# Inverse roots of the keys' norms from GpSimd to ScalarE, context rows all normalised on GpSimd, with a new order table for every engine, in a two-block attention network

## The chip, the cores and the metric

The kernel runs on one core of a Trainium2 chip. The metric is the device time of one execution in microseconds (us). Four compute engines run side by side, each through its own queue in order: TensorE (PE), VectorE (DVE), ScalarE (ACT) and GpSimd (POOL). SyncE (SP) issues the DMAs. Engines wait for one another on semaphores.

## The reference

The input `x` is 512 tokens (8 batches of 64) of width 128, with a context of 8 x 1601 rows of width 128. Six blocks follow one another, each added to `x` after a layer norm:

1. `_L0_xattn_ref`: four layers of self-attention, cross-attention to the first context rows, and a gated feed-forward part.
2. `_L0_attn_ref`: messages, with a sigmoid of pairwise products.
3. `_L0_ffn_ref`: one small product.
4. `_L1_xattn_ref`: the tokens attend to the 1601 context rows of their batch and to themselves.
5. `_L1_attn_ref`: causal attention with rotary positions.
6. `_L1_ffn_ref`: eight experts, all computed, two kept per token.

The change is in `_L1_xattn_ref`. What it needs of the context rows:

```python
xn = layernorm(x, ln_x_g, ln_x_b)          # x is the context here: (row - mean) * rsqrt(var + eps)
kv = jnp.concatenate([xn @ W_kv, ln @ W_kv], axis=1)
kn = rmsnorm(k, k_gamma)                   # k / max(norm(k) / 8, 1e-8) for each of 2 heads of 64
sim = einsum(qn, kn); masked; attn = softmax(sim); out = attn @ v
```

## The kernel before, in words

All work is cut into named pieces. Token tiles are t = 0..3 (128 tokens each). A context batch i = 0..7 has thirteen tiles of 128 rows, in groups g = 0..3 of 4, 4, 4 and 1 tiles (`CG`). In a piece's name the first number is the layer, batch or expert and the second the tile or group. The table `PIECES` says which engine runs a piece, and the table `PLACES` gives each piece its place in that engine's queue: `Order` sorts by it, and the engine runs the pieces one after another. `PLACED` gives the PSUM bank of each PE piece, and `WARM` the number of matmuls on a zero tile (L727) that PE runs ahead of a piece. A piece waits for others by `after(engine, od, piece, i, g)`, and `step` makes an engine wait for its own last instruction. Layer 4 of `turn1`, `project`, `scores` and so on is the attention of `_L1_attn_ref`.

For one context batch the chain of pieces is:

- DVE `c_moments` (mean and variance of each row, done during the layers, L1507 and L1510), then POOL `c_power` (L1719 to L1722: 1/sqrt(var + eps) and minus mean times that).
- POOL `c_normed` (groups 0 and 1, L1733 and L1735) and ACT `c_spread` (groups 2 and 3, one ACTIVATE for each of five tiles, L1291) write the normalised rows to `xh[i % 3]`. Both wait until `sum_ctx` of batch i-3 has read that buffer.
- PE `c_turn` (transposes, L1061), ACT `c_turned` (L1301), PE `c_keys` (L1067), ACT `c_squares` (L1307), DVE `c_sums` (L1514), POOL `c_rnorm` (L1738 and L1739): the inverse norm of every key in `rk`. Beside it PE `c_scores` (L1077 and L1079), which needs `c_turned` only.
- DVE `c_scaled` multiplies scores by `rk` (L1518), DVE `c_top` and `top` take the maximum over the batch (L1525 to L1538), PE `top_turn` (L1085), DVE `top_row` and `top_diag` (L1541, L1545), PE `top_spread` (L1089), DVE `shifted` (L1550), ACT `weights` (exponential, L1311), PE `sum_ctx` (weighted sum of `xh`, L1094), then `u_turn` and `heads`.

`load_context` loads batch b (SP) when `c_normed` and `c_spread` of batch b-2 are through. The rule that decides whether a piece is the first of its kind:

```python
def leads(od, p, i, g):
    if SHAPE[p][1] == T:
        return (p, i, g) in od.first
```

`od.first` holds the earliest group of each piece and batch, and T is 4.

## Time and profile before

| | us |
|---|---|
| median of 3 runs | 488.76 (488.09 to 489.97) |
| the profiled execution, its own time | 495.46 |
| its span from first to last instruction | 493.5 |
| PE busy | 455.0 (92%) |
| DVE busy | 366.1 (74%) |
| ACT busy | 280.3 (57%) |
| POOL busy | 217.8 (44%) |

The busy time of an engine is the sum of its instructions' durations. The span is cut three ways below: layers and most of the messages up to 280 us, context and the causal attention up to 430 us, the experts after that. A clock of 1.00 is TensorE at its higher level, 2.4 GHz, and 0.50 is 1.2 GHz. "POOL rk L1739" is the pow instruction that writes tile `rk`.

### The profile page before, as it was taken

To read this page: it belongs to the slowest core of one execution; us is meant where nothing else is said; L and a number is where in the kernel's file an instruction comes from. 1 tells how busy PE (TensorE), PEld (TensorE's weight loads), DVE (VectorE), ACT (ScalarE), POOL (GpSimd) and SP (SyncE) were. 2 spreads that over 40 slices of the span, in tenths; PEclk is the share of its full clock that TensorE was granted. 3 is DMA by queue.
4 is the path that set the end of the run, shared out by engine and by line. 5 is a ranking of instruction groups with operands and counts; after the bars stand their busy time and mean duration, and the time that the engine had idled before them with its cause. 6 is when DMAs were issued, how large, how long until landed. Compare 5 with 4: busy or idle time off the path is not lost.

```text
span 493.5 us, 14858 instructions
## 1 busy us (share of the span) xinstructions
PE 455.0 (92%) x5683; PEld 392.6 (80%) x5705; DVE 366.1 (74%) x1053; ACT 280.3 (57%) x752; POOL 217.8 (44%) x350
## 2 busy tenths in 40 slices
PE   8998998999879989999789999978999899999997
PEld 3666876777769767889779899867889798789996
DVE  5888899669874897565752669978788996865553
ACT  3688487767766787662562544836657644443131
POOL 4703474534452475211652449966667751110000
PEclk9999799999988998999989999979999999999999
DMA  7921222030201400000420037030100000000000
GB/s 206 386 83 41 68 79 66 3 107 20 98 30 35 139 3 2 2 3 3 149 70 1 4 114 298 17 117 2 68 2 2 0 1 1 3 1 4 0 2 26
DMA packets 10321, 27.84 MB, mean 56 GB/s; under 512 B 1391, under 2 KB 5381, under 8 KB 9990
## 3 DMA queue, kind: packets, MB, share of 16 engines
q1 hardware_dynamic: 10246, 26.82, 16.1%
q8 instruction: 49, 0.80, 0.7%
q14 instruction: 26, 0.21, 0.1%
HBM read 26.55 MB, written 0.26 MB: 54 GB/s over the span
## 4 chain that ended last, share of the span: by engine, by line
PE 58%; DVE 20%; POOL 8%; ACT 6%; issue 6%; DMA 1%; SPq 0%; DVEq 0%; POOLq 0%; ACTq 0%
PE ps L1164 6%; PE ps L1155 6%; PE ps L1008 3%; PE ps L1094 3%; PE ps L939 3%; PE ps L879 3%; PE ps L1079 3%; PE ps L972 2%; POOL rk L1739 2%; PE ps L869 2%; PE ps L1067 2%; DVE mx L1381 2%; POOL rsx L1720 2%; PE ps L999 2%; DVE own L1386 2%
## 5 line engine op out<-in xcount | busy, mean ns | idle before, releaser
L1682 POOL TENSOR_TENSOR rstd<-ss,par 128x1 f32<-128x1 f32 x52 | 28.7, 557 | 60.0 <-ACT sq L1184 59.9
L1739 POOL TENSOR_TENSOR rk<-rk,par 128x8 f32<-128x8 f32 (+1 forms) x32 | 46.0, 1438 | 2.7
L1212 ACT ACTIVATE own<-own 128x512 f32<-128x512 f32 x56 | 35.2, 628 | 17.4 <-DVE own L1412 8.7
L1381 DVE TENSOR_REDUCE mx<-ps 128x8 f32<-128x512 f32 x40 | 27.3, 682 | 5.0 <-PE ps L861 4.7
L1079 PE MATMUL ps<-own,xnT 128*128 128x128 f32 x208 | 29.6, 282 | 0.9 <-DVE ssq L1486 0.3
L1164 PE MATMUL ps<-we,own 128*128 128x128 f32 x256 | 30.3, 276 | 0.0
L1672 POOL TENSOR_TENSOR qk<-own 128x128 f32<-128x128 f32 x40 | 18.6, 470 | 25.9 <-DVE own L1374 25.4
L1164 PEld LDWEIGHTS ps<-we,own 128*128 128x128 f32 x256 | 29.7, 192 | 0.4
L1155 PE MATMUL ps<-hT,we 128*128 128x256 f32 x128 | 29.7, 381 | 0.2 <-issue 0.2
L1079 PEld LDWEIGHTS ps<-own,xnT 128*128 128x128 f32 x208 | 28.5, 197 | 1.4 <-issue 0.5
L1342 ACT ACTIVATE own<-ps,we 128x256 f32<-128x256 f32 x32 | 13.4, 470 | 28.4 <-PE ps L1155 22.5
L1695 POOL TENSOR_TENSOR rstd<-mv,par 128x1 f32<-128x1 f32 x24 | 5.1, 213 | 54.0 <-DVE mv L1441 54.0
L1067 PE MATMUL ps<-xw,xnT 128*128 128x128 f32 x208 | 28.5, 280 | 0.1
L1386 DVE TENSOR_TENSOR own<-ps,mx 128x512 f32<-128x512 f32 x40 | 27.5, 688 | 1.2
L1094 PE MATMUL ps<-xh,own 128*128 128x130 f32 x208 | 26.7, 277 | 0.1
L1374 DVE SCALAR_TENSOR_TENSOR own<-ps,wa,trig 128x128 f32<-128x128 f32 x80 | 23.0, 343 | 4.8 <-PE ps L838 4.6
L1301 ACT ACTIVATE xnT<-ps,xw 128x512 f32<-128x512 f32 (+1 forms) x32 | 21.6, 696 | 8.4 <-PE ps L1061 5.2
L1067 PEld LDWEIGHTS ps<-xw,xnT 128*128 128x128 f32 x208 | 25.3, 191 | 1.2 <-ACT xnT L1301 0.3
L1155 PEld LDWEIGHTS ps<-hT,we 128*128 128x128 f32 x128 | 23.5, 191 | 3.2 <-issue 0.4
L869 PE MATMUL ps<-cf,own 128*128 128x128 f32 x160 | 24.2, 281 | 1.6 <-DVE rec L1561 1.0
L879 PEld LDWEIGHTS ps<-vblk,own 128*64 128x64 f32 x640 | 21.2, 137 | 5.4 <-issue 2.0
L1216 ACT COPY own<-ps 128x512 f32<-128x512 f32 x40 | 22.9, 582 | 4.6 <-PE ps L869 4.3
(247 smaller groups left out, 1309.0 us busy)
## 6 DMA issues: line engine op xcount, KB each, us to landing
cx<-ctx_in SPq DMA_DIRECT2D x14, 768.0 KB
we<-we_in SPq DMA_DIRECT2D x8, 514.0 KB, 6.8
wc<-wc_in SPq DMA_DIRECT2D x4, 768.5 KB, 6.0
wa<-wa_in SPq DMA_DIRECT2D x5, 387.0 KB, 3.0
uvT<-uvT_in SPq DMA_DIRECT2D x1, 1024.0 KB, 10.1
uv<-uv_in SPq DMA_DIRECT2D x1, 1024.0 KB, 10.5
...
```

The costliest lines, as they stand in the source:

```text
L869: last = nc.tensor.transpose(bank[:, P * j:P * j + P], pr[:, g, 512 * k + P * j:512 * k + P * j + P], ident)
L879: last = nc.tensor.matmul(bank[L * b:L * b + L, 18 * j:18 * j + 18], pts[:, g, P * j + L * b:P * j + L * b + L], vblk[:, g, b, j, :, :], s ...
L1067: last = nc.tensor.matmul(bank[:, P * j:P * j + P], xnT[n % 3][:, P * j:P * j + P], xw[:, X_K:X_K + P], start=True, stop=True)
L1079: last = nc.tensor.matmul(bank[:, P * j:P * j + P], xnT[n % 3][:, P * j:P * j + P], columns(qp[t][:, k, :, :]), start=False, stop=True, sk ...
L1094: last = nc.tensor.matmul(bank[:, 0:D + 2], sT[i][:, c, :], xh[i % 3][:, c, :], start=(c == 0), stop=(c == CT - 1))
L1155: last = nc.tensor.matmul(bank[:, 2 * P * c:2 * P * c + 2 * P], we[:, i, W_1 + P * c:W_1 + P * c + P], columns(hT[:, 2 * g:2 * g + 2, :]), ...
L1164: last = nc.tensor.matmul(bank[:, P * k:P * k + P], hid[g][i % 2][:, c, P * k:P * k + P], we[:, i, W_2 + P * c:W_2 + P * c + P], start=(c ...
L1212: done(nc.scalar.activation(pr[:, g, a:a + 512], sd[:, g, a:a + 512], ACT.Exp), p)
L1381: done(nc.vector.tensor_reduce(mx[:, g, 8 * k:8 * k + 8].rearrange("p (r i) -> p r i", i=4), quad(od, i, g)[:, 2 * k:2 * k + 2, :, :], AX, ...
L1386: done(nc.vector.tensor_tensor(sd[:, g, 512 * k:512 * k + 512].rearrange("p (r i k) -> p r i k", i=4, k=L), quad(od, i, g)[:, 2 * k:2 * k ...
L1682: done(nc.gpsimd.tensor_tensor(rstd[:, t:t + 1], ss[:, t:t + 1], par[:, 1:2], ALU.pow), p)
L1739: done(nc.gpsimd.tensor_tensor(rk[:, n, 0:2 * w], rk[:, n, 0:2 * w], par[:, 1:2].to_broadcast([P, 2 * w]), ALU.pow), p)
```

## The change

`c_rnorm` moves from POOL (max with a floor, then pow) to ACT: `Ln`, a wait for it, then `Exp` with scale -0.5. The max with the floor moves to DVE, behind `c_sums`, which waits for its own reduce first. Ahead of the first root of each batch stands a load of ACT's function tables. `c_spread` is dropped: POOL's `c_normed` does all four groups, with two instructions for each. `c_power` writes only the inverse root of the variance. `load_context` waits for `c_normed` alone. All tables of places and banks are new, and `WARM` holds 30 matmuls at fifteen places where it held 29 at twelve.

```diff
@@ PIECES, the pieces of ACT, then of POOL
-        "c_spread": (B, 2), "c_turned": GROUPED, "c_squares": GROUPED, "weights": GROUPED, "sum_taken": BATCHED, "u_turned": BATCHED,
+        "c_turned": GROUPED, "c_squares": GROUPED, "c_rnorm": GROUPED, "weights": GROUPED, "sum_taken": BATCHED, "u_turned": BATCHED,
-        "l_rnorm": TILED, "x_blank": TILED, "x_clear": (1, 1), "c_power": BATCHED, "c_normed": (B, 2), "c_rnorm": GROUPED, "a_power": TILED, "e_power": TILED,
+        "l_rnorm": TILED, "x_blank": TILED, "x_clear": (1, 1), "c_power": BATCHED, "c_normed": GROUPED, "a_power": TILED, "e_power": TILED,
@@ pe_context
             elif p == "c_turn":
                 bank = take(pe, od, p, i, g)
-                if g < 2:
-                    after(pe, od, "c_normed", i, g)
-                else:
-                    after(pe, od, "c_spread", i, g - 2)
+                after(pe, od, "c_normed", i, g)
@@ act_context
-            elif p == "c_spread":
-                if i >= 3:
-                    after_all(act, od, "sum_ctx", i - 3)
-                elif i in (1, 2):
-                    after(act, od, "x_clear", 0)
-                after(act, od, "c_power", i)
-                if i >= 2:
-                    act.wait_ge(s["ctx_loaded%d" % (i % 2)], 32 * (B // 2 + i // 2))
-                for c in CG[g + 2]:
-                    last = nc.scalar.activation(xh[i % 3][:, c, 0:D], cx[i % 2][:, c, :], ACT.Identity, scale=rsx[:, i, c:c + 1],
-                                                bias=mrx[:, i, c:c + 1])
-                done(last, p)
+            elif p == "c_rnorm":
+                if leads(od, p, i, g):
+                    nc.scalar.preload_act_table_set("natural_log_exp_and_others")
+                after(act, od, "c_sums", i, g)
+                roots = rk[:, n, 0:2 * width(g)]
+                step(act, "scalar_step", nc.scalar.activation(roots, kss[:, n, 0:2 * width(g)], ACT.Ln))
+                done(nc.scalar.activation(roots, roots, ACT.Exp, scale=-0.5), p)
@@ dve_context
             elif p == "c_sums":
                 after(dve, od, "c_squares", i, g)
-                done(nc.vector.tensor_reduce(kss[:, n, 0:2 * w], ksq[n % 2][:, 0:P * w].rearrange("p (a d) -> p a d", d=XD), AX, ALU.add), p)
+                squares = kss[:, n, 0:2 * w]
+                step(dve, "vector_step", nc.vector.tensor_reduce(squares, ksq[n % 2][:, 0:P * w].rearrange("p (a d) -> p a d", d=XD), AX, ALU.add))
+                done(nc.vector.tensor_scalar(squares, squares, RMS_FLOOR, None, ALU.max), p)
@@ pool_piece
                 step(pool, "pool_step", nc.gpsimd.tensor_tensor(rsx[:, i, :], mvx[:, i, :, 1], par[:, 0:1].to_broadcast([P, CT]), ALU.add))
-                step(pool, "pool_step", nc.gpsimd.tensor_tensor(rsx[:, i, :], rsx[:, i, :], par[:, 1:2].to_broadcast([P, CT]), ALU.pow))
-                step(pool, "pool_step", nc.gpsimd.tensor_tensor(mrx[:, i, :], mvx[:, i, :, 0], rsx[:, i, :], ALU.mult))
-                done(nc.gpsimd.tensor_scalar(mrx[:, i, :], mrx[:, i, :], -1.0, None, ALU.mult), p)
+                done(nc.gpsimd.tensor_tensor(rsx[:, i, :], rsx[:, i, :], par[:, 1:2].to_broadcast([P, CT]), ALU.pow), p)
...
-            elif p == "c_rnorm":
-                after(pool, od, "c_sums", i, g)
-                step(pool, "pool_step", nc.gpsimd.tensor_scalar(rk[:, n, 0:2 * w], kss[:, n, 0:2 * w], RMS_FLOOR, None, ALU.max))
-                done(nc.gpsimd.tensor_tensor(rk[:, n, 0:2 * w], rk[:, n, 0:2 * w], par[:, 1:2].to_broadcast([P, 2 * w]), ALU.pow), p)
@@ PLACES (every line of the table differs; the one of c_normed) and WARM
-    "c_normed": (130, 127, 157, 152, 159, 158, 189, 190, 192, 191, 202, 204, 208, 207, 223, 222),
+    "c_normed": (130, 127, 128, 132, 159, 166, 156, 161, 168, 164, 163, 169, 187, 188, 185, 184, 192, 191, 190, 189, 196, 195, 194, 193, 197, 198,
+        200, 199, 204, 203, 201, 202),
-    ("turn1", 0, 0): 7, ("down", 0, 2): 3, ("turn3", 0, 3): 1, ("turn_1", 1, 2): 2, ("turn2", 1, 1): 1, ("turn1", 2, 0): 2,
-    ("out", 2, 0): 4, ("project_q", 3, 0): 1, ("turn_1", 3, 2): 2, ("turn3", 3, 0): 2, ("out", 3, 3): 2, ("c_turn", 7, 0): 2,
+    ("weigh0", 0, 2): 3, ("cturn_o", 0, 0): 2, ("cscores", 1, 1): 1, ("weigh0", 1, 3): 2, ("scores", 2, 0): 2, ("cscores", 2, 0): 2,
+    ("turn2", 2, 1): 2, ("cturn", 2, 2): 2, ("turn_1", 3, 1): 3, ("weigh0", 3, 1): 2, ("turn_1", 3, 2): 2, ("turn2", 3, 2): 2,
+    ("l_turn", 0, 0): 2, ("sum_ctx", 5, 0): 2, ("e_turn", 0, 0): 1,
```

In the changed kernel the lines that the prediction speaks of are L1058 (`c_turn`), L1064 (`c_keys`), L1074 and L1076 (`c_scores`), L1082 (`top_turn`), L1091 (`sum_ctx`), L1286 (`c_turned`), L1292 (`c_squares`), L1295 (table load), L1298 and L1299 (`c_rnorm`), L1303 (`weights`), L1507 and L1508 (`c_sums`), L1725 and L1727 (`c_normed`).

On ACT, in the kernel before, at the exponentials of the first two context batches (L1311), with the `c_spread` of batches 3 and 4 (L1291) among them:

```order
L1311 ACTIVATE own<-own 128x512 x2
L1311 ACTIVATE own<-own 128x256
L1311 ACTIVATE own<-own 128x512
L1291 ACTIVATE xh0<-cx1,mrx,rsx 128x128
L1311 ACTIVATE own<-own 128x512
L1316 COPY un_x0<-ps 128x130
L1291 ACTIVATE xh0<-cx1,mrx,rsx 128x128 x4
L1320 ACTIVATE utx0<-ps,xw 128x128
L1316 COPY un_x1<-ps 128x130
L1291 ACTIVATE xh1<-cx0,mrx,rsx 128x128 x5
L1320 ACTIVATE utx1<-ps,xw 128x128
```

On ACT, in the changed kernel, at the roots of batches 0 and 1:

```order
L1248 COPY own<-ps 128x1024
L1292 ACTIVATE ksq1<-ps 128x128
L1292 ACTIVATE ksq0<-ps 128x512
L1298 ACTIVATE rk<-kss 128x2
L1299 ACTIVATE rk<-rk 128x2
L1295 ACT_TABLE_LOAD
L1298 ACTIVATE rk<-kss 128x8
L1299 ACTIVATE rk<-rk 128x8
L1263 ACTIVATE hT<-ps,xw 128x128
L1267 ACTIVATE own<-ps 128x256
```

The five-tile ACTIVATEs on `xh` are gone from this queue, and a table load with pairs on `rk` stands among the squares.

On POOL, in the kernel before, from the roots of batch 2 to the normalisation of batches 3 and 4:

```order
L1738 TENSOR_SCALAR rk<-kss 128x8
L1739 TENSOR_TENSOR rk<-rk,par 128x8
L1738 TENSOR_SCALAR rk<-kss 128x2
L1739 TENSOR_TENSOR rk<-rk,par 128x2
L1733 TENSOR_TENSOR xh0<-cx1,mvx 128x4x128
L1735 TENSOR_TENSOR xh0<-xh0,rsx 128x4x128
L1733 TENSOR_TENSOR xh0<-cx1,mvx 128x4x128
L1735 TENSOR_TENSOR xh0<-xh0,rsx 128x4x128
L1733 TENSOR_TENSOR xh1<-cx0,mvx 128x4x128
L1735 TENSOR_TENSOR xh1<-xh1,rsx 128x4x128
L1733 TENSOR_TENSOR xh1<-cx0,mvx 128x4x128
L1735 TENSOR_TENSOR xh1<-xh1,rsx 128x4x128
```

On POOL, in the changed kernel, at the normalisation of batch 3 (L1709 and L1710 are the roots of the queries' norms, one of tile 3, one of tile 2):

```order
L1709 TENSOR_SCALAR rqk<-ssq 128x4
L1710 TENSOR_TENSOR rqk<-rqk,par 128x4
L1725 TENSOR_TENSOR xh0<-cx1,mvx 128x128
L1727 TENSOR_TENSOR xh0<-xh0,rsx 128x128
L1725 TENSOR_TENSOR xh0<-cx1,mvx 128x4x128
L1727 TENSOR_TENSOR xh0<-xh0,rsx 128x4x128
L1709 TENSOR_SCALAR rqk<-ssq 128x4
L1710 TENSOR_TENSOR rqk<-rqk,par 128x4
L1725 TENSOR_TENSOR xh0<-cx1,mvx 128x4x128
L1727 TENSOR_TENSOR xh0<-xh0,rsx 128x4x128
L1725 TENSOR_TENSOR xh0<-cx1,mvx 128x4x128
L1727 TENSOR_TENSOR xh0<-xh0,rsx 128x4x128
```

The roots have left this queue, and each batch now has four groups where it had two. From here on the changed queue holds nothing but such pairs down to batch 7.

On PE, in the kernel before, where batch 7 is first transposed (L1061 on `xh1`):

```order
L1077 MATMUL ps<-sel,notm 128x512
L1079 MATMUL ps<-own,xnT2 128x128 x4
L1089 MATMUL ps<-dg1,ones 128x128
L1077 MATMUL ps<-sel,notm 128x128
L1079 MATMUL ps<-own,xnT0 128x128
L853 MATMUL ps<-cb 64x4x32 x16
L861 MATMUL ps<-own,qk 64x256 x8
L727 MATMUL ps<-still 128x512 x2
L1061 MATMUL ps<-cf,xh1 128x128 x8
L1067 MATMUL ps<-xw,xnT1 128x128 x4
L1061 MATMUL ps<-cf,xh1 128x128 x4
```

On PE, in the changed kernel, the last rows ahead of the transposes of batch 7. Ahead of the first row shown stand, back to the last `sum_ctx` of batch 4, one `o_turn`, one `o_project`, one `u_turn`, a one-tile and two four-tile `c_scores`, and a four-tile and a one-tile `c_keys`:

```order
L1074 MATMUL ps<-sel,notm 128x512
L1076 MATMUL ps<-own,xnT2 128x128 x4
L1074 MATMUL ps<-sel,notm 128x128
L1076 MATMUL ps<-own,xnT0 128x128
L1119 MATMUL ps<-xw,oTx1 128x128
L1082 MATMUL ps<-cf,mxp1 128x128
L1103 MATMUL ps<-rs40,eye2 64x4
L1108 MATMUL ps<-xw,utx0 64x64
L1109 MATMUL ps<-qk,own 64x64
L1108 MATMUL ps<-xw,utx0 64x64
L1109 MATMUL ps<-qk,own 64x64
L1058 MATMUL ps<-cf,xh1 128x128 x13
```

The first row of `sum_ctx` of batch 5 (L1094 on `xh2`) stands three rows behind this in the kernel before, between transposes and keys of batch 7. In the changed kernel the thirteen transposes of batch 7 stand in one block ahead of all sums of batches 5 and 6, and the causal attention of tile 0 comes behind them instead of ahead (it began between the keys of batch 3 before).

## Rows read from the trace of the kernel before

**Rows 1.** The page: busy time and share of the span of each engine.
```profile
PE 455.0 (92%) x5683; PEld 392.6 (80%) x5705; DVE 366.1 (74%) x1053; ACT 280.3 (57%) x752; POOL 217.8 (44%) x350
```

**Rows 2.** Windows: busy time by engine (instructions), granted clock, DMA share, GB/s.
```profile
0.00:280.00 280.00, 255.68 (x3960) 211.59 (x3970) 206.99 (x622) 178.40 (x511) 124.61 (x222) 0.96 0.22 70
280.00:430.00 150.00, 139.23 (x1247) 125.88 (x1253) 125.35 (x327) 83.37 (x195) 90.23 (x121) 0.98 0.14 52
430.00:493.50 63.50, 60.06 (x493) 55.18 (x491) 33.75 (x106) 18.51 (x48) 2.98 (x7) 1.00 0.02 6
```

**Rows 3.** Windows around 48 us, the same columns.
```profile
46.00:48.00 2.00, 0.93 (x7) 0.64 (x6) 1.96 (x8) 1.53 (x6) 0.67 (x2) 1.00 0.71 211
48.00:50.00 2.00, 2.00 (x23) 1.77 (x21) 1.85 (x14) 1.23 (x5) 0.31 (x1) 0.55 0.10 24
```

**Rows 4.** Windows around 326 us, the same columns.
```profile
324.00:326.00 2.00, 0.29 (x1) 0.18 (x1) 1.76 (x8) 0.33 (x1) 1.02 (x2) 0.67 0.62 181
326.00:328.00 2.00, 1.73 (x9) 1.90 (x10) 1.69 (x5) 0.00 (x0) 1.59 (x4) 0.50 0.57 229
```

**Rows 5.** Chain that ended last, in order of time: start, duration, what.
```profile
293.97 1.68 POOL rk L1739
...
301.80 1.67 POOL rk L1739
...
396.95 0.89 PE ps L1067 x8
398.01 1.05 PE ps L1079 x8
...
439.98 0.87 PE ps L869 x8
```

**Rows 6.** Groups of instructions on POOL, shapes apart: count, busy us, mean ns.
```profile
L1739 POOL TENSOR_TENSOR rk<-rk,par 128x8 f32<-128x8 f32 x24 | 40.1, 1672 | 2.0
...
L1735 POOL TENSOR_TENSOR xh<-xh,rsx 128x512 f32<-128x512 f32 x16 | 17.6, 1103 | 1.3
L1733 POOL TENSOR_TENSOR xh<-cx,mvx 128x512 f32<-128x512 f32 x16 | 17.6, 1097 | 1.6 <-PE ps L1096 1.4
...
L1738 POOL TENSOR_SCALAR rk<-kss 128x8 f32<-128x8 f32 x24 | 6.3, 261 | 19.9 <-DVE kss L1514 18.7
L1739 POOL TENSOR_TENSOR rk<-rk,par 128x2 f32<-128x2 f32 x8 | 5.9, 734 | 0.7
...
L1712 POOL TENSOR_TENSOR x<-x,bout 128x128 f32<-128x128 f32 x4 | 1.9, 465 | 1.1 <-DMA sel<-sel_in 1.1
```

**Rows 7.** Groups of instructions on ACT, shapes apart.
```profile
L1291 ACT ACTIVATE xh<-cx,mrx,rsx 128x128 f32<-128x128 f32 x40 | 16.6, 486 | 6.8 <-PE ps L1096 5.3 <-POOL mrx L1722 1.5
...
L2030 ACT ACT_TABLE_LOAD x1 | 1.3, 1283 | 0.7 <-PEq L2134 0.7
...
L1332 ACT ACTIVATE gex<-gsh 128x16 f32<-128x16 f32 x2 | 0.4, 216 | 1.8 <-DVE gsh L1591 1.7
```

**Rows 8.** Groups of instructions on DVE, shapes apart.
```profile
L1529 DVE TENSOR_TENSOR mxr<-mxr,own 128x256 f32<-128x256 f32 x16 | 9.4, 587 | 0.6
...
L1605 DVE TENSOR_TENSOR picked<-rank,top 128x16 f32<-128x16 f32 x4 | 0.7, 175 | 0.1
```

**Rows 9.** Waits of PE's weight loads: us in total, times, longest.
```profile
PEld ps L1089 <- DVE dg L1545: 2.2, 3, 1.2
PEld ps L1085 <- DVE rec L1561: 2.2, 1, 2.2
PEld ps L1061 <- DVE own L1518: 2.1, 3, 1.0
```

**Rows 10.** Timeline of DVE at 377 and 386 us: start, duration, instruction.
```profile
377.00 0.43 DVE L1529 TENSOR_TENSOR mxr<-mxr,own 128x256 f32<-128x256 f32 x1
...
386.19 1.15 DVE L1529 TENSOR_TENSOR mxr<-mxr,own 128x256 f32<-128x256 f32 x1
```

**Rows 11.** Timeline of POOL near 386 us.
```profile
385.95 1.10 POOL L1735 TENSOR_TENSOR xh<-xh,rsx 128x512 f32<-128x512 f32 x1
```

More of the change, by code:

```diff
@@ L418 @@
[L418 to L427 removed]
+    "mem_kp": "22",
+    "mem_vp": "32232310",
+    "turn1": "01333111613145601715",
+    "project": "40500302616157505507",
+    "project_q": "21011131423065611163",
+    "values": "11020213537214020115",
+    "scores": "44444400444400040000",
@@ new lines @@
+    "turn0": "31300474131171520540",
+    "turn_1": "10032454102245745741",
+    "weigh0": "33100666101176530741",
+    "turn_o": "00100666101077567541",
+    "out": "00120661131076570545",
+    "turn2": "2201557210046624",
+    "qc": "2201777710047620",
+    "cscores": "4444000044400444",
+    "cturn": "3323740010154335",
+    "cweigh": "3323740010454330",
+    "cturn_o": "1244567030771235",
+    "cout": "2244571000751536",
+    "turn3": "1452732233541025",
+    "gate": "0462442442640044",
+    "down": "5042270225642534",
@@ new lines @@
+    "m_turn": "6414",
+    "m_across0": "6002",
+    "m_across1": "2666",
+    "m_along0": "4002",
+    "m_along1": "6226",
+    "m_pairs0": "2404",
+    "m_pairs1": "2660",
+    "m_sums0": "6220",
+    "m_sums1": "2402",
+    "m_back": "4456",
+    "f_turn": "6714",
+    "f_mm": "6714",
+    "l_turn": "0756",
+    "l_qkv": "0516",
+    "q_turn": "0540",
+    "qk0": "4470",
+    "qk1": "5246",
+    "l_scores": "5546",
+    "bwv_p": "5",
+    "c_turn": "12345627462012413263060377600723",
+    "c_keys": "12364627475017476747070037304525",
@@ L428 @@
+    "c_scores": "64774627272456403063636711030765",
+    "top_turn": "77520126",
+    "top_spread": "33024347",
+    "sum_ctx": "30127761",
+    "u_turn": "23123761",
+    "heads": "03126643",
+    "o_turn": "3123",
+    "o_project": "2227",
+    "e_turn": "2544",
+    "e_logits": "24",
+    "e_cho": "70",
+    "e_b2": "75",
+    "e_up": "2642042646022066",
+    "e_down": "2644640553025312",
 }
 WARM = {
-    ("turn1", 0, 0): 7, ("down", 0, 2): 3, ("turn3", 0, 3): 1, ("turn_1", 1, 2): 2, ("turn2", 1, 1): 1, ("turn1", 2, 0): 2,
```

427 lines of the change are left out of this document (184 added, 243 removed), and 50 rows, old and new, of the table PLACES.

## The prediction

> **What bounds the kernel now.** I read the page's busy line first: PE is busy 455.0 of 493.5 us [rows 1]. Next are windows by stage [rows 2], because an average hides where the other 38.5 us lie. Up to 280 us PE idles 24.3 us (280 - 255.68), from 280 to 430 us it idles 10.8 us (150 - 139.23), and in the expert part 3.4 us. In the expert part DVE, ACT and POOL are about half busy or less, so nothing that this change touches is worth anything there.
>
> The second loss is the clock. From 46 to 48 us PE does 0.93 us of work in two, and the granted clock of the next two is 0.55 [rows 3]. From 324 to 326 us it does 0.29 us, and the next two run at 0.50, the level of 1.2 GHz [rows 4]. Over the stages that is 0.04 x 280 = 11.2 us and 0.02 x 150 = 3.0 us of clock given away [rows 2]. So an idle microsecond can cost more than itself, and a gap that appears or closes moves the total by some microseconds.
>
> Third is the context part itself, from 280 to 430 us, where the change acts. There DVE is busy 125.35 of 150 us, POOL 90.23, ACT 83.37 [rows 2]. POOL's pow for eight values per row takes 1.67 us, and the chain of waits passes through it in a burst that begins at 293.97 us and has its last piece at 301.80 us [rows 5, 6]. Meanwhile PE waited for what comes behind: its weight loads waited 2.1 us for scaled scores (L1518), 2.2 us for the diagonal of maxima (L1545) and 2.2 us for `h_recip` (L1561) [rows 9]. That is 6.5 of the 10.8 idle us, all behind DVE's queue.
>
> **The change, part by part.**
>
> *Roots leave POOL.* 24 pows at 1.67 us and 8 at 0.73 us, with their max instructions at 0.26 us, are 40.1 + 5.9 + 6.3 + 8 x 0.26 = 54.4 us [rows 6]. None of it is PE's time. What it gives PE is latency: a group's root took 0.26 + 1.67 = 1.9 us after `c_sums`, in a queue it shared with the normalisation of later batches. Behind it waited `c_scaled`, so the bank of `c_scores`, so PE.
>
> *Roots on ACT.* The trace has no `Ln`. The nearest row is the exponential of 16 values, 0.216 us [rows 7], so 64 instructions cost 64 x 0.216 = 13.8 us, and a root takes some 0.5 us with its wait between the two instead of 1.9. Bounds: not under the 0.216 us for the pair, not over the one pow that it replaces. I take 0.5.
>
> *Table loads.* `leads` is true for the earliest group of every batch, so eight loads stand in the queue. The one load in the trace takes 1.283 us [rows 7]: 8 x 1.28 = 10.3 us of ACT. They are issued ahead of the wait for `c_sums`, so where ACT would wait there anyway they cost nothing. The cover is ACT's idle time, 150 - 83.4 = 67 us of the stage. Without it, behind a load stand `c_turned` and `weights`, for which PE waits. Bounds 0 and 10.3 us, and I take 0.5, since ACT is idle nearly half the time.
>
> The trace's only load stands at the start, with no work ahead of it. The Trainium skill's page "ScalarE: Activation LUTs" (What ACT_TABLE_LOAD costs) gives the same 1283 ns for the load and adds about 1380 ns of drain, 2.66 us for every switch to another set. By it eight loads would be 21 us of ACT if a reload of the same set drained as a switch does, and no run here shows that yet.
>
> *Spread leaves ACT.* 40 ACTIVATEs, 16.6 us, go [rows 7]. ACT's balance is 13.8 + 10.3 - 16.6 = +7.5 us on 83.4 of 150: no bound.
>
> *All thirteen tiles on POOL.* For eight batches, one more four-tile group (2 x 1.10 us) and one single tile (2 x 0.465 us, by the row of a 128x128 tensor pair) are 17.6 + 7.4 = 25.0 us [rows 6]. `c_power` loses two small instructions. POOL's balance is about 25 - 54 = -29 us. But a batch now takes 3 x 2.2 + 0.93 = 7.5 us of POOL, where two groups took 4.4 us with ACT beside them. The sharpest place is batch 7: its first group is POOL's last, and all four wait for the last `sum_ctx` of batch 4. PE has in between three four-tile `c_scores` at 1.05, one four-tile `c_keys` at 0.89, and for the one-tile pieces, turns, projections and heads about 2.4 us (a transpose is 0.87 / 4 = 0.22) [rows 5], together 6.4 us. So `c_turn` of batch 7 should wait about 1 us. Bounds 0 and 2.
>
> *DVE's added max.* 32 instructions of a few values per row, each behind its own reduce. The nearest is 0.175 us [rows 8]: 5.6 us. Bounds: 0 if it hides behind other waits, 32 x 0.25 = 8 us with the wait for the reduce.
>
> *Contention.* At 386.19 us a DVE maximum of two SBUF tensors takes 1.15 us where the same line took 0.43 at 377.00. It ends 0.29 us after POOL's tensor pair, which ran from 385.95 to 387.05 us [rows 10, 11]. The 16 of that line average 0.587 us [rows 8]. POOL's large pairs grow from 35.2 us by 25.0 us, a factor of 1.7. Against 0.43 us undisturbed, that line loses 16 x 0.16 = 2.6 us now. All such lines of the stage lose perhaps double, so the added part is about 0.7 x 5 = 3.6 us of DVE. The Trainium skill's "GPSIMD Engine Reference" (Specifications) says that GpSimd's SBUF interfaces are shared with VectorE, with contention for instructions of two SBUF inputs; by that rule, the trace agrees.
>
> *The new order.* It moves the attention of tile 0 from inside batch 3 to the end of the context part, and moves every piece of the layers. The layers' work is the same, with one dummy matmul more. I can't price an order from a profile of another one, so I take 0 for 0 to 280 us, with bounds of -6 and +6: about half of its 11.2 us of clock either way.
>
> **The sum**, against the profiled execution: earlier `c_scaled` wins two thirds of the 6.5 us of waits, -4.3. The idle stretch near 324 us and its slow clock shrink, of 3.0 us given away half, -1.5. The wait at batch 7 adds 1.0. DVE's 5.6 + 3.6 = 9.2 us fall on an engine that idles 24.6 of 150 us, so a sixth to a quarter shows, +1.8. Table loads, +0.5. Together -2.5 us: span 491.0 us, profiled time 493.0 where it was 495.46 (its own time is 2 us over its span). The median of the runs is 488.76, 1.4% below the profiled one, so I predict **486.3 us**.
>
> **The rivals.**
>
> 1. *Forecast, a small gain*, 483 to 488 us: 0.42.
> 2. *The order closes gaps in the layers too.* For it speaks that 24 idle us and 11 us of clock lie there, more than twice what lies in the context part. Against it, the change touches no duration there. Two slow stretches fewer would give 7 us: 480 us. 0.14.
> 3. *PE holds the time, and the saved latency isn't on its path*: PE is at 93% in the stage, and gaps shift from one wait to another. 488.8 us, 0.20.
> 4. *DVE becomes the bound of the context part.* DVE would be busy 125.4 + 9.2 = 134.6 of 150 us. If its idle time (it waits for PE and ACT in turn) stays above half of today's 24.6 us, nothing is lost. If all of it stays, the stage is 9.2 us longer, and with half of that and one new slow stretch of 3 us the time is 488.8 + 4.6 + 3 = 496 us; at the mild end 492. The added max stands between `c_sums` and everything else in that queue, which speaks for it. 0.16.
> 5. *Table loads stand in PE's way.* It decides if more than about three of eight are met with `c_turned` or `weights` due. Six so met at 1.28 us, less the gain: 488.8 - 2.5 + 7.7 = 494 us. 0.08.
>
> By the figure of 2.66 us for a switch, from the page "ScalarE: Activation LUTs" of the Trainium skill (What ACT_TABLE_LOAD costs), six such loads would cost 16 us and the time would be 502 us; the chance of that lies within rival 5's.
>
> **How the numbers follow.** What a measurement of this kernel can tell from no change is about 0.5%, 2.4 us. Rival 1 is faster by more than that with about 0.7, rival 2 always: 0.29 + 0.14 + 0.02 from rival 3 = 0.45. Same: 0.13 from 1 and 0.16 from 3, 0.29. Slower: rivals 4 and 5 and 0.02 from 3, 0.26. The likeliest case's own range is 483 to 488. The range 479 to 496 leaves out the far ends of rivals 2 and 4.
>
> **What would show it.** Windows by stage: PE idle in the context part down from 10.8 to 7 or 8 us, and no stretch at 0.50 there. The group of L1298 and L1299 at 0.2 us each, eight loads at 1.28 us. PE's wait at L1058 ahead of batch 7 near 1 us. DVE maxima (L1525 to L1538 of before) with a higher mean. Wrong would be the prediction if PE's idle time or granted clock before 280 us moves by more than 3 us, or if DVE or ACT releases PE for more than the 6.5 us of before.

## The result, and the profile after

The changed kernel takes **507.62 us** (median of 4 runs, 506.21 to 509.44), the kernel before beside it 489.37 us (median of 4). The ratio on record is 1.0315, 95% interval 1.026 to 1.037; the quotient of these two medians is 1.037, so the loss is 15 to 18 us, depending on which runs of the kernel before it is held against. An execution can fall well above the others of its kernel (497.85 us beside 491.35 us); the ratios in this document leave such runs out, the medians do not, so quotients of medians can differ from them by some tenths of a per cent. I had forecast 486.3 us and a range of 479 to 496. The prediction was wrong, in sign and in size. The profiled execution of the changed kernel took 508.1 us, span 505.8 us.

Its busy line, and its windows by the stages of [rows 1, 2] (us of the window, then busy us of each engine with its instructions, then the granted clock):

```profile
PE 456.0 (90%) x5682; PEld 392.1 (78%) x5706; DVE 373.5 (74%) x1085; ACT 288.7 (57%) x784; POOL 184.2 (36%) x302
```

```profile
0.00:280.00 280.00, 249.98 (x3861) 206.82 (x3877) 205.28 (x622) 172.40 (x492) 125.44 (x214) 0.98 0.21 70
280.00:430.00 150.00, 135.41 (x1254) 121.70 (x1259) 126.94 (x328) 92.53 (x229) 53.55 (x76) 0.97 0.15 52
```

PE is busy as long, 456.0 us against 455.0, at the same mean clock (0.975 and 0.972), so against the first profile the loss is idle time: 30.0 us before 280 us where there were 24.3, and 14.6 us from 280 to 430 where there were 10.8, and the context part does not end at 430 any more. The prediction had named a shift of more than 3 us in PE's idle time before 280 us as a sign that it is wrong, and that sign is there. POOL's busy time fell by 33.6 us, near the sum's 29 and `c_power`'s two small instructions. No run shows a gain from it.

The groups of the instructions that the change added or moved, and of two of the maxima (busy us, mean ns of one, idle us before them and who ended it):

```profile
L1725 POOL TENSOR_TENSOR xh<-cx,mvx 128x512 f32<-128x512 f32 x24 | 25.8, 1075 | 24.5 <-PE ps L1093 24.4
L1727 POOL TENSOR_TENSOR xh<-xh,rsx 128x512 f32<-128x512 f32 x24 | 26.1, 1088 | 1.9
L1295 ACT ACT_TABLE_LOAD x8 | 10.3, 1283 | 0.1
L1298 ACT ACTIVATE rk<-kss 128x8 f32<-128x8 f32 x24 | 4.9, 205 | 4.1 <-DVE kss L1508 4.0
L1298 ACT ACTIVATE rk<-kss 128x2 f32<-128x2 f32 x8 | 1.6, 200 | 5.2 <-DVE kss L1508 5.2
L1299 ACT ACTIVATE rk<-rk 128x8 f32<-128x8 f32 x24 | 5.0, 209 | 0.8
L1508 DVE TENSOR_SCALAR kss<-kss 128x2 f32<-128x2 f32 x8 | 2.2, 280 | 0.3
L1523 DVE TENSOR_TENSOR mxr<-mxr,own 128x256 f32<-128x256 f32 x16 | 9.3, 580 | 0.6
L1522 DVE TENSOR_TENSOR mxr<-mxr,own 128x256 f32<-128x256 f32 x16 | 8.7, 544 | 0.8
```

The durations are near those that I had put into the sum (the max of DVE is 0.22 us in the mean where I had 0.175). What I had wrong is what they do in their place. One stretch shows three of the costs at once. First POOL's timeline from 354 us (start, duration), then DVE's, then ACT's, with idle time and its releaser in brackets:

```profile
354.55 1.10 POOL L1727 TENSOR_TENSOR xh<-xh,rsx 128x512 f32<-128x512 f32 x1
355.62 1.22 POOL L1725 TENSOR_TENSOR xh<-cx,mvx 128x512 f32<-128x512 f32 x1
356.92 1.11 POOL L1727 TENSOR_TENSOR xh<-xh,rsx 128x512 f32<-128x512 f32 x1
...
359.06 1.04 POOL L1725 TENSOR_TENSOR xh<-cx,mvx 128x512 f32<-128x512 f32 x1
```

```profile
354.86 1.08 DVE L1522 TENSOR_TENSOR mxr<-mxr,own 128x256 f32<-128x256 f32 x1
355.97 1.15 DVE L1523 TENSOR_TENSOR mxr<-mxr,own 128x256 f32<-128x256 f32 x1
357.22 1.08 DVE L1522 TENSOR_TENSOR mxr<-mxr,own 128x256 f32<-128x256 f32 x1
358.34 0.50 DVE L1523 TENSOR_TENSOR mxr<-mxr,own 128x256 f32<-128x256 f32 x1
...
359.07 1.05 DVE L1508 TENSOR_SCALAR kss<-kss 128x2 f32<-128x2 f32 x1
...
362.07 0.17 DVE L1508 TENSOR_SCALAR kss<-kss 128x8 f32<-128x8 f32 x1
```

```profile
360.16 0.20 ACT L1298 ACTIVATE rk<-kss 128x2 f32<-128x2 f32 x1 [2.86 <-DVE kss L1508]
360.39 0.20 ACT L1299 ACTIVATE rk<-rk 128x2 f32<-128x2 f32 x1
360.50 0.58 ACT L1292 ACTIVATE ksq<-ps 128x512 f32<-128x512 f32 x1
361.10 1.28 ACT L1295 ACT_TABLE_LOAD   x1
362.39 0.21 ACT L1298 ACTIVATE rk<-kss 128x8 f32<-128x8 f32 x1
```

Four maxima in a row run beside POOL's tensor pairs, three of them at 1.08 to 1.15 us. The added max with the floor, two values per row, takes 1.05 us beside POOL's next one; on eight values and with POOL idle it takes 0.17 us. ACT stands 2.86 us at the root that waits for it, with everything behind it in its queue. Then comes a table load of 1.28 us, and the next root begins 0.01 us after it. The chain of waits of the same kernel goes through all of it (start, us, what). It passes through six of the eight table loads, those at 281.33, 310.23, 350.55, 361.10, 373.47 and 398.29 us, 7.7 us in all:

```profile
354.86 1.09 DVE mxr L1522
...
355.97 1.16 DVE mxr L1523
...
359.07 1.06 DVE kss L1508
360.16 0.21 ACT rk L1298
...
361.10 1.28 ACT L1295
```

### The profile page after: what moved, and what is told of

Same layout as the page of the kernel before. It is cut to its first block, busy times and chain, and to the rows that moved or that the text cites. A ratio compares the mean times of both kernels' runs of the same rounds, so it can differ in the third digit from the quotient of the medians.

```text
span 505.8 us, 14861 instructions
## 1 busy us (share of the span) xinstructions
PE 456.0 (90%) x5682; PEld 392.1 (78%) x5706; DVE 373.5 (74%) x1085; ACT 288.7 (57%) x784; POOL 184.2 (36%) x302
## 4 chain that ended last, share of the span: by engine, by line
PE 61%; DVE 17%; ACT 11%; issue 5%; POOL 2%; DMA 2%; SPq 1%; DVEq 0%; ACTq 0%; POOLq 0%
PE ps L1161 6%; PE ps L1152 6%; PE ps L939 3%; PE ps L879 3%; PE ps L869 3%; PE ps L972 2%; PE ps L1091 2%; PE ps L1064 2%; PE ps L1008 2%; PE ps L1076 2%; PE ps L944 2%; PE ps L951 2%; PE ps L832 2%; PE ps L928 2%; ACT L1295 2%
## 5 line engine op out<-in xcount | busy, mean ns | idle before, releaser
L1725 POOL TENSOR_TENSOR xh<-cx,mvx 128x512 f32<-128x512 f32 (+1 forms) x32 | 30.3, 945 | 33.5 <-PE ps L1093 33.4
L1076 PE MATMUL ps<-own,xnT 128*128 128x128 f32 x208 | 29.9, 286 | 1.7 <-ACT un_x L1308 0.9
L1727 POOL TENSOR_TENSOR xh<-xh,rsx 128x512 f32<-128x512 f32 (+1 forms) x32 | 29.4, 919 | 2.5
L1076 PEld LDWEIGHTS ps<-own,xnT 128*128 128x128 f32 x208 | 29.2, 201 | 1.1
L1064 PE MATMUL ps<-xw,xnT 128*128 128x128 f32 x208 | 28.8, 287 | 1.4 <-ACT xnT L1286 1.4
L1064 PEld LDWEIGHTS ps<-xw,xnT 128*128 128x128 f32 x208 | 25.8, 196 | 2.7 <-ACT xnT L1286 1.2
L1091 PE MATMUL ps<-xh,own 128*128 128x130 f32 x208 | 26.5, 278 | 0.6 <-ACT own L1303 0.3
L1286 ACT ACTIVATE xnT<-ps,xw 128x512 f32<-128x512 f32 (+1 forms) x32 | 21.4, 696 | 8.7 <-PE ps L1058 7.4
L879 PE MATMUL ps<-vblk,own 128*64 128x18 f32 x640 | 23.4, 212 | 3.3 <-ACT own L1213 2.8
L1091 PEld LDWEIGHTS ps<-xh,own 128*128 128x128 f32 x208 | 24.6, 191 | 2.0 <-ACT own L1303 0.9
## 6 DMA issues: line engine op xcount, KB each, us to landing
uvT<-uvT_in SPq DMA_DIRECT2D x1, 1024.0 KB, 10.6
wm<-wm_in SPq DMA_DIRECT2D x1, 512.0 KB, 6.2
```

The source lines that it names most:

```text
L879: last = nc.tensor.matmul(bank[L * b:L * b + L, 18 * j:18 * j + 18], pts[:, g, P * j + L * b:P * j + L * b + L], vblk[:, g, b, j, :, :], s ...
L1064: last = nc.tensor.matmul(bank[:, P * j:P * j + P], xnT[n % 3][:, P * j:P * j + P], xw[:, X_K:X_K + P], start=True, stop=True)
L1076: last = nc.tensor.matmul(bank[:, P * j:P * j + P], xnT[n % 3][:, P * j:P * j + P], columns(qp[t][:, k, :, :]), start=False, stop=True, sk ...
L1091: last = nc.tensor.matmul(bank[:, 0:D + 2], sT[i][:, c, :], xh[i % 3][:, c, :], start=(c == 0), stop=(c == CT - 1))
L1725: step(pool, "pool_step", nc.gpsimd.tensor_tensor(part, cx[i % 2][:, tiles, :], mvx[:, i, tiles, 0].unsqueeze(2).to_broadcast(shape), ALU. ...
L1727: done(nc.gpsimd.tensor_tensor(part, part, rsx[:, i, tiles].unsqueeze(2).to_broadcast(shape), ALU.mult), p)
```

## The experiments

Each ratio is against the kernel before on the same chip, with its 95% interval. The edits are given in short form; where pieces change engine, their places in the tables change with them. "Old order" and "new order" are the tables of places, banks and warming matmuls of the kernel before and of the changed one. I held three theories. **A**: the new order costs the time. **B**: the changed operations do, through table loads, DVE's longer work and roots behind other work in ACT's queue. **E**: POOL's tensor pairs stretch DVE's work, and PE waits for that. Parts of B are called C (table loads), D (the start, a part of A in truth) and F (the floor) in the expectations.

### A second profile of the kernel before

No edit.

> The kernel before, unchanged, for a second profile of it: the first was of an execution of 495.5 us where the median is 489 to 491, so a stretch in which the changed kernel seems level with it may in truth be up to 5 us behind. Theory A and B both expect about 490 us; if this profile is near 490, the curve of equal work tells where those 5 us lay (dips of the granted clock in the layers).

493.1 us, span 491.0 us. It replaces the first profile below, whose execution (495.46 us) was further above the median.

### Order against operations: three runs beside the two kernels

```diff
 e1:  code of before;  -PLACES, PLACED, WARM of before  +those of the changed kernel
 e2:  changed code;    -PLACES, PLACED, WARM            +those of before
 e16: as e2, and
-                if leads(od, p, i, g):
+                if (i, g) == (0, 0):
                     nc.scalar.preload_act_table_set("natural_log_exp_and_others")
```

> The operations of the kernel before (roots by two operations on GpSimd, six of thirteen tiles of a batch normalised on ScalarE, no later table loads) in the new order: the new numbers of places, banks and warming matmuls, with the roots put on GpSimd's queue where the sums ended in the trace of the changed kernel, and the two pieces of ScalarE's normalisation where GpSimd's stood. Theory A, the new order costs the time: 505 to 510 us, ratio 1.03 to 1.04. Theory B, the changed operations cost it: 487 to 492 us, ratio within 0.995 to 1.005. Between them (495 to 501) both have a share.

> The changed kernel's operations in the order, banks and warming matmuls of the kernel before; the roots stand on ScalarE's queue where the sums ended in the trace of before (those of batch 0 behind the last tanh), the tiles that GpSimd took over right behind its others of that batch. Theory A (order): 487 to 491 us, ratio 0.995 to 1.005. Theory B (operations: eight table loads of 1.28 us, longer VectorE work, roots behind other work on ScalarE): 502 to 510 us, ratio 1.025 to 1.04. With the two kernels known this gives all four corners: if the costs only add, this run and the one in the new order with the old operations have gains that sum to 18 us.

> The run of the changed operations in the old order (1.047) with one table load in place of eight; the pair to the changed kernel with one load in the new order (1.022). If the new order is worth something for its own operations, this stands above it: 1.030 to 1.042 (505 to 512 us). If the new order is worse for any operations, as it was for the old ones, this stands at or below 1.022 (502 us).

| | old order | new order |
|---|---|---|
| old operations | 1 | 1.0645 (1.057 to 1.072), 524.64 us |
| new operations, eight loads | 1.0472 (1.041 to 1.054), 513.71 us | 1.0315, the changed kernel |
| new operations, one load | 1.0348 (1.029 to 1.040), 508.94 us | 1.0219 (1.017 to 1.027), 502.05 us, run e3 below |

Neither A nor B alone. The operations cost 4.7% in the order that was there. With them the new order stands 1.6% lower (1.3% with one load), and with the old ones it is bad. (The expectation of e1 speaks of six tiles of a batch on ACT; it is five.) My e1, e2 and e16 place the exchanged pieces by one trace and are no tuned orders, so their corners are upper bounds.

### Single parts of the change

e3 is the load's edit above in the changed kernel. e4 moves the start:

```diff
 e4, changed kernel
-POOL: x_zero, mem_copy, pow1 x3, base ...            +POOL: x_zero, pow1 x3, base x3, pow1, base, mem_copy ...
-PE: turn1, turn1, mem_vp 2 0 ...                      +PE: 7 dummies, turn1 x3 ... mem_vp 2 0 (and mem_v on DVE) later
 e6, kernel before
-  ACT: c_spread (B, 2)    POOL: c_normed (B, 2)      +  POOL: c_normed GROUPED
 e7, kernel before
-  POOL: c_rnorm           DVE: sum                   +  ACT: c_rnorm, Ln and Exp, one load    DVE: sum, floor
 e15, kernel before
-  POOL: floor, pow        DVE: sum                   +  POOL: pow                             DVE: sum, floor
 e17, as e7, the floor without DVE
-  ACT.Ln, and on DVE tensor_scalar(squares, squares, RMS_FLOOR, None, ALU.max)
+  ACT.Ln, bias=par[:, 3:4]     # a column that holds RMS_FLOOR
```

> The changed kernel with the table of natural logarithm and exponential loaded once, ahead of batch 0's first root, and not for each of the eight batches: seven loads of 1283 ns, 9.0 us of ScalarE, are gone. Rival C, table loads are a main part: 498 to 501 us. Theory A (order): loads of batches 2 to 7 lie mostly in ScalarE's slack, 503.5 to 507 us. If they were wholly hidden: 507 to 508.

> The changed kernel with the start laid out as before: on GpSimd the copy of the memory behind the first powers of layer 0, the value projection that needs it and VectorE's copy of that later, and seven warming matmuls ahead of the first transposition. Rival D, the 2.9 us that the changed kernel lies behind at 10 us of work are lost for good: 504 to 505.5 us. If waits later swallow it: 506.5 to 508 us. The clock granted in 0 to 25 us should rise from 0.86 and the first transposition end near 10 us.

> One part alone, in the old order: GpSimd normalises all thirteen tiles of a batch (ScalarE's two pieces are gone, their tiles stand right behind GpSimd's others), the roots stay on GpSimd by its two operations, no table load, no floor on VectorE. The run with both parts in the old order was 22.5 us slower than before. If the tiles are what it could not bear: 505 to 515 us. If the roots behind other work on ScalarE are: 489 to 495 us.

> The other part alone, in the old order: roots by logarithm and exponential on ScalarE (one table load, behind the last tanh), their floor on VectorE; the tiles are normalised as before on both engines. If the roots are what the old order could not bear: 500 to 510 us. If the tiles are: 488 to 493 us. If the two only hurt together, both of these runs lie under 495.

> The kernel before with one part of the change alone: the floor of the sums is an operation of VectorE behind each sum (32 of 0.20 us and a wait on itself) and no longer one of GpSimd (32 of 0.25 us); all else is as before. By the run of the changed kernel without the floor (3 us less, within the two intervals): ratio 1.003 to 1.008. If it is hidden: 0.998 to 1.002.

> The run with the roots alone moved in the old order (1.012), with the floor added as the logarithm's bias on ScalarE (the sum plus 1e-16, in place of the larger of the two), so that VectorE has no more work than before. If costs add: 1.002 to 1.006 (493 to 495 us), the roots' move as such costs nothing. If it is under 0.997, GpSimd's 54 us less are worth something and this version beats both kernels. If over 1.009, the roots in ScalarE's queue cost time themselves.

| run | median us | ratio |
|---|---|---|
| e3, changed kernel, one load | 502.05 | 1.0219 (1.017 to 1.027) |
| e4, changed kernel, start as before | 507.11 | 1.0292 (1.022 to 1.037) |
| e6, tiles alone | 507.65 | 1.0264 (1.018 to 1.035) |
| e7, roots alone, floor on DVE | 498.66 | 1.0121 (1.004 to 1.020) |
| e15, floor alone | 496.59 | 1.0089 (1.006 to 1.012) |
| e17, roots alone, free floor | 498.19 | 1.0146 (1.010 to 1.019) |

Seven loads, 9.0 us of ACT, cost 1.0% in the new order and 1.2% in the old (1.0472 to 1.0348), about 5 to 6 us. The start costs nothing that this measurement shows; its interval would hide 3 us. The floor alone costs 0.9%. Tiles and roots moved alone cost 2.6 and 1.2%, and their sum is near the 3.5% of both together in that order. The roots were to be a gain. With the floor taken off DVE (e17) they still cost 1.5%, so e17's forecast that costs add did not hold: e7 and e17 can't be told apart, and by e17 the move of the roots as such costs 1.0 to 1.9%.

Why the saved latency was worth little is seen in DVE's waits ahead of the scaled scores, 275 to 440 us, in e5, the changed kernel, e3 and e6, in this order:

```profile
L1518 DVE TENSOR_TENSOR own<-ps,rk 128x512 f32<-128x512 f32 (+1 forms) x32 | 18.7, 585 | 5.3 <-PE ps L1079 3.4 <-POOL rk L1739 1.6
```

```profile
L1512 DVE TENSOR_TENSOR own<-ps,rk 128x512 f32<-128x512 f32 (+1 forms) x32 | 18.2, 584 | 2.6 <-ACT rk L1299 1.5 <-PE ps L1076 1.1
```

```profile
L1512 DVE TENSOR_TENSOR own<-ps,rk 128x512 f32<-128x512 f32 (+1 forms) x32 | 18.2, 583 | 0.9 <-PE ps L1076 0.9
```

```profile
L1496 DVE TENSOR_TENSOR own<-ps,rk 128x512 f32<-128x512 f32 (+1 forms) x32 | 18.7, 586 | 7.2 <-POOL rk L1715 4.8 <-PE ps L1069 2.0
```

Before, DVE waited 1.6 us here for POOL's roots, though e5's chain of waits spends 8.6% of this window, some 14 us, in the pow: DVE had other work nearly until each root came. In the changed kernel it waits 1.5 us for ACT's roots, and with one load (e3) not at all. So the quick root won about the 1.6 us that there were, and the loads took them again. In e6, whose profiled execution was the longest of its four (512.46 us), it waits 4.8 us, for roots that stand behind thirteen tiles in POOL's queue. And ACT, where the roots now stand, has to wait for the sums in order. Two rows of e17 for the same window, and the second's counterpart in e5:

```profile
L1309 ACT ACTIVATE rk<-kss,par 128x8 f32<-128x8 f32 (+1 forms) x30 | 8.9, 295 | 8.3 <-DVE kss L1517 8.3
L1517 DVE TENSOR_REDUCE kss<-ksq 128x8 f32<-128x512 f32 (+1 forms) x30 | 16.9, 574 | 4.2 <-ACT ksq L1303 4.0
```

```profile
L1514 DVE TENSOR_REDUCE kss<-ksq 128x8 f32<-128x512 f32 (+1 forms) x30 | 16.8, 572 | 2.3 <-ACT ksq L1307 2.0
```

POOL waited 20.2 us for the same sums in e5. ACT's 8.3 us, and 9.2 in the changed kernel (4.0 and 5.2 in the groups above), hold up what stands behind them: DVE waits 4.0 us for the squares where it waited 2.0 (4.7 in the changed kernel). What was won at the roots is lost there. The rest of e17's loss does not show as waits of PE. The window from 275 to 440 us in e17, then in e5:

```profile
275.00:440.00 165.00, 154.93 (x1388) 138.41 (x1389) 132.36 (x345) 101.25 (x270) 41.65 (x64) 0.94 0.13 47
```

```profile
275.00:440.00 165.00, 154.45 (x1473) 139.41 (x1485) 135.30 (x353) 90.53 (x212) 92.67 (x126) 0.97 0.13 47
```

PE idles 10.1 us in e17 and 10.6 in e5. What differs is the granted clock, 0.94 against 0.97, which is 5.0 us of clock over the window, and the two executions lie 4 us apart. So what e17 loses in this window is clock and not idle time. How the roots' place in ACT's queue leads to that, one profile each does not show, and no run isolates it.

### POOL's normalising and DVE's maxima

```diff
 e8 (changed kernel, one load) and e11 (kernel before)
-  done(tensor_tensor(part, part, rsx[...].to_broadcast([P, w, D]), ALU.mult), p)
+  few = part[:, :, 0:8]
+  done(tensor_tensor(few, few, rsx[...].to_broadcast([P, w, 8]), ALU.mult), p)
 e9 (changed kernel, one load) and e10 (kernel before)
-  tensor_tensor(part, cx, mean, ALU.subtract); tensor_tensor(part, part, rsx, ALU.mult)
+  for c in CG[g]: last = tensor_scalar(xh[:, c, 0:D], cx[:, c, :], mean[c], rsx[c], ALU.subtract, ALU.mult)
 e13 (changed kernel, one load)
-  POOL: c_normed GROUPED                             +  POOL: c_normed (B, 2)   ACT: c_spread (B, 2)
 e14 (kernel before)
-  POOL: c_normed (B, 2)   ACT: c_spread (B, 2)       +  POOL: c_normed (B, 1)   ACT: c_spread (B, 3)
```

> The changed kernel with one table load (502.05 us) and with the second of GpSimd's two operations of each normalised piece cut to 8 of 128 columns: it leaves out most of the scaling by the root of the variance, so about 29 us of 57 us of GpSimd's work beside VectorE are gone. Rival E, GpSimd's work in SBUF stretches VectorE's maxima and this holds PE: 496 to 499.5 us, and the mean of the maxima falls from 0.54 to 0.58 us towards 0.45. Otherwise 501 to 503 us.

> Control for the run that halved the normalising of the changed kernel (10 us less): the same cut in the kernel before, the second operation of each normalised piece on 8 of 128 columns; it leaves out most of the scaling by the root of the variance of GpSimd's eight tiles. If GpSimd's normalising costs the changed kernel what it did not cost before: ratio 0.995 to 1.000 here (0 to 2.5 us). If any kernel would gain 10 us by the cut: ratio near 0.98, and then that gain says nothing of the change.

> The changed kernel with one table load, and the normalisation on GpSimd by one operation a tile that subtracts the mean and multiplies by the root at once (13 operations of 128 columns a batch, with the two numbers as per-partition scalars) in place of two operations of up to 512 columns a piece that read two tensors each. Theory E (GpSimd's two-tensor operations stretch VectorE's maxima from 0.43 or 0.58 us to 1.1 us, and those maxima hold PE): 491 to 496 us and maxima near 0.29 to 0.47 us in the mean, as in the run with half of the normalising. If any operation of GpSimd stretches them alike: 497 to 501 us. If GpSimd's operation of a tile costs over 0.6 us each: 502 us or more.

> The kernel before, untouched but for the same edit: GpSimd normalises its eight tiles of a batch by one operation a tile. Nothing of the change is in it. Theory E: also here maxima are stretched (1.15 us at 386 us), so 2 to 5 us are to be had: ratio 0.99 to 0.996. If VectorE's stretch cost before nothing that PE saw: ratio 0.998 to 1.002.

> The new order and the changed kernel's roots (one table load, floor on VectorE), but groups 2 and 3 of each batch (five tiles) are normalised on ScalarE again, queued where GpSimd's pieces began in the trace of the changed kernel with one load. By the slope of the two halving runs (about 0.5 us for each us of GpSimd's normalising) the 22 us that leave GpSimd are worth 10 us: 490 to 495 us, if ScalarE's 16.6 us are hidden. If ScalarE has no room at those places in the new order: 505 to 520 us, like the run of the new order with both old operations (524.6), and then that run's loss was these pieces.

> The other way than the change, in the kernel before and its order: group 1 of each batch (four tiles) moves from GpSimd to ScalarE, queued where GpSimd's piece began, so GpSimd normalises four of thirteen tiles and ScalarE nine (13 us more of ScalarE, 17 us less of GpSimd). If the stretch by GpSimd is what counts: ratio 0.980 to 0.992. If ScalarE's time counts as much: 0.995 to 1.01. If ScalarE's queue is what the new order suffered from: above 1.015.

| run | median us | ratio |
|---|---|---|
| e8, new, one load, half normalising | 493.63 | 1.0008 (0.998 to 1.004) |
| e11, before, half normalising | 486.62 | 0.9874 (0.983 to 0.992) |
| e9, new, one load, one operation a tile | 510.27 | 1.0411 (1.035 to 1.047) |
| e10, before, one operation a tile | 494.46 | 1.0061 (1.003 to 1.009) |
| e13, new, one load, five tiles on ACT | 507.22 | 1.0309 (1.025 to 1.037) |
| e14, before, nine tiles on ACT | 493.94 | 1.0039 (1.000 to 1.008) |

e8 and e11 leave out most of the scaling by the inverse root of the variance. Halving wins 2.1% in the changed kernel with one load (from 1.0219) and 1.3% in the kernel before, so a good part of e8's gain is to be had in any version and isn't the change's. The maxima of e3, then of e8:

```profile
L1522 DVE TENSOR_TENSOR mxr<-mxr,own 128x256 f32<-128x256 f32 x16 | 9.5, 592 | 0.8
L1532 DVE TENSOR_TENSOR mxp<-mxp,sm 128x128 f32<-128x128 f32 x8 | 4.6, 573 | 0.3
```

```profile
L1522 DVE TENSOR_TENSOR mxr<-mxr,own 128x256 f32<-128x256 f32 x16 | 8.0, 502 | 0.8
L1532 DVE TENSOR_TENSOR mxp<-mxp,sm 128x128 f32<-128x128 f32 x8 | 2.3, 292 | 0.3
```

With one operation a tile most of the stretch is gone (the longest of the first line is 607 ns where e3 has 1210) though POOL is busy longer; e9's POOL group and two of its maxima:

```profile
L1724 POOL TENSOR_SCALAR xh<-cx,mvx,rsx 128x128 f32<-128x128 f32 x104 | 85.7, 833 | 15.2 <-PE ps L1093 15.0
L1522 DVE TENSOR_TENSOR mxr<-mxr,own 128x256 f32<-128x256 f32 x16 | 7.2, 447 | 0.8
L1532 DVE TENSOR_TENSOR mxp<-mxp,sm 128x128 f32<-128x128 f32 x8 | 2.8, 347 | 0.3
```

So the stretch is real and comes from POOL's operations on two tensors. But e9 is 1.9% slower than e3, not faster: a tile takes 0.83 us where a quarter of two operations of 1.08 took 0.54, and `c_turn` gets its rows later: PE waits 4.7 us for them, and in e3's list of waits there is none of that kind. Of my theory E the stretch of DVE is shown. That the stretch alone holds PE is not: e9 gained nothing without it, and in e14 17 us less of tensor pairs for 13 us more of ACT changed nothing worth having. Both runs trade the stretch for another cost, so its own price is open. e13 stands 0.9% above e3, so in the new order the tiles are rather better on POOL, though the two intervals touch.

### The floor in the new order

```diff
 e12 (changed kernel, one load), e18 the same with the floor as the logarithm's bias
-  done(nc.vector.tensor_scalar(squares, squares, RMS_FLOOR, None, ALU.max), p)
```

> The changed kernel with one table load and without VectorE's second operation of each sum, the floor at 1e-16 (32 operations of 0.20 us and a wait of VectorE on itself each, 6 to 8 us of VectorE); it leaves out that floor. Theory F, the added VectorE work is a part of the loss: 497 to 500 us. If it is hidden: 501 to 503 us.

> The changed kernel with one table load and the floor as the logarithm's bias: the run without a floor (1.016) in a form that computes it. 1.012 to 1.019 (498 to 501 us); that leaves 1.2 to 1.9% that neither the table loads nor VectorE's added operation explain.

500.36 us, 1.016 (1.009 to 1.023), and 498.76 us, 1.0185 (1.012 to 1.025): both under e3's 1.0219, by 0.6 and 0.3%, which the intervals alone don't settle. With e15 (0.9%) the floor is worth 2 to 4 us.

### Where in the run the time goes

PE's work is the same in all, 419 us when each kind of piece is given its median duration. So I read from each profile when 240 us of it were done (in the first context batches), and how long the rest took, up to PE's last instruction (3.4 to 5.5 us before the end of the span). The durations weigh the work, and another choice of weights moves the columns by up to some 12 us but their differences by about 1 us:

| profile | its own time | 240 of 419 us done at | the rest |
|---|---|---|---|
| before, e5 | 493.1 | 291.6 | 195.7 |
| e15, floor on DVE | 494.4 | 289.4 | 199.7 |
| e7, roots, floor | 497.8 | 291.2 | 199.9 |
| e16, old order, one load | 510.4 | 296.1 | 206.5 |
| e2, old order, eight loads | 512.0 | 296.5 | 209.5 |
| changed kernel | 508.1 | 297.9 | 202.9 |
| e3, one load | 502.7 | 297.2 | 199.8 |
| e12, no floor | 500.8 | 300.3 | 194.7 |
| e18, free floor | 496.4 | 295.2 | 195.5 |

Read the last column down the changed kernel: 202.9, less the loads 199.8, less the floor 195.5, and that is before's 195.7. **Behind this point the loss of the changed kernel is no larger than what the table loads and the floor account for.** What the roots and the tiles cost in the old order, 1.5% and 2.6%, does not show here in the new order. This rests on one profile each. e18's execution was 2.4 us under its median, but e12's was 0.4 above and reads 194.7. A single profile is not sure to some microseconds: e4, with the changed kernel's context operations and order and an execution of 512.67 us, takes 5.6 us longer for the rest than the changed kernel does. The other part is in the middle column. At 145 of 419 us, in the layers, the eleven profiles with the old order stand at 182.9 to 189.8 us (median 186.0), the nine with the new order at 191.9 to 199.1 (195.2): 9 us later, though no duration there changed. It is the order and not the operations: e2 and e16, with the new operations in the old order, are among the first, and e1, with the old operations in the new order, among the second. At 240 us the medians are still 291.8 against 297.9, 6 us. The first 100 us and the next 90 of the changed kernel, then of e5:

```profile
0.00:100.00 100.00, 85.81 (x1072) 64.31 (x1076) 78.64 (x263) 63.07 (x189) 45.04 (x80) 0.93 0.34 115
100.00:190.00 90.00, 80.59 (x1160) 65.67 (x1166) 69.67 (x226) 64.50 (x200) 39.01 (x64) 1.00 0.18 59
```

```profile
0.00:100.00 100.00, 90.75 (x1209) 67.49 (x1212) 83.33 (x276) 68.46 (x206) 48.64 (x91) 1.00 0.36 119
100.00:190.00 90.00, 79.94 (x1159) 65.75 (x1165) 72.39 (x241) 65.77 (x211) 46.69 (x79) 0.98 0.17 55
```

In the first 100 us PE is busy 4.9 us less and is granted 0.93 where e5 had 1.00, 7 us of clock. Behind that nothing more is lost: to 190 us PE is busy 0.7 us more and its clock is 1.00 against 0.98. So the layers' loss arises in their first 100 us. With the start laid out as before (e4) the clock of the first 50 us rises from 0.93 to 1.00, but that of the next 50 is 0.90 where it was 0.93, and at 100 of the 419 us of work e4 is level with the changed kernel; so the start alone is not the lasting loss. Which piece is late I didn't isolate: the two orders can't be cut and joined there, because tiles pass from the layers to the messages at different times.

## Why the prediction was wrong, point by point

- **The new order, taken as 0 with bounds of 6 us either way.** The step that failed most by size: 6 us at the end of the messages, at the edge of the bound, a term for which the sum had nothing. I had said that I can't price an order from another's profile, and then put the middle into the sum. The later loss in the layers is seen in nine profiles against eleven.
- **Table loads, +0.5.** Mis-sized: 1.0%, about 5 us, in e3, and 6 us in the old order. I counted ACT's idle time of the stage (67 us) as cover. But a load ahead of a root is placed where the root is due, and six of the eight are on the chain of waits at their full length. Rival 5 had this mechanism, the six loads and their 7.7 us, at a chance of 0.08; taking seven away gave 5 to 6 us.
- **DVE, 9.2 us of which 1.8 show.** The max with the floor took 7.0 us in 32 (I had 5.6), and costs 0.3 to 0.9% (e12, e18, e15), 2 to 4 us. It isn't spread over DVE's idle time either: it stands between each sum and its root, and was 1.05 us long where POOL ran a tensor pair. The stretch of the maxima was forecast rightly: their five lines took 27.4 us in e5 and 30.7 in the changed kernel, 3.3 more where I had 3.6. One line's mean went from 438 to 544 ns, another's (640 in e5) did not rise.
- **Earlier `c_scaled`, -4.3.** The sign failed. DVE had waited for roots 1.6 us ahead of `c_scaled`, in the kernel before too, a row that I should have read before booking 4.3. I took two thirds of PE's waits behind DVE for waits behind the root. Moving the roots alone cost 1.2 to 1.5% (e7, e17).
- **Tiles on POOL, +1.0 at batch 7.** `c_turn` of batch 7 began at 390.79 us without a wait, so the wait wasn't there. What the move costs elsewhere I had not seen: 2.6% in the old order (e6), where DVE waits 4.8 us for roots behind POOL's longer queue. In the new order DVE has no such wait (e3).
- **The clock, -1.5.** No gain: PE did 0.54 us of work from 324 to 326 us, where DVE was busy 1.96 and POOL 1.92 us, and the next two were at 0.61. Over 280 to 430 us the clock is 0.97 where it was 0.98.
- **The sum.** Measured +15 to +18 us for -2.5: loads 5, floor 2 to 4, the order before the context part 6. That makes 13 to 15 us. By the ratio 1.0315 the loss is 15.4 us, and the profiles of e5 and the changed kernel lie 15.0 us apart; what is missing up to 18 us lies within the intervals of these ratios (some 3 us each).

Beside the order, which had no price at all, the failed terms have one root. Each was a duration, or a wait, times a guessed share. For the loads and the max the share came from the stage's idle time, and for `c_scaled` from waits whose cause was not read. It ought to have come from what stands next to the new instruction in its queue.
